# First attention of a two-layer block: rotary exchange by DMA instead of a second projection, and the maxima in two groups of two

## The reference, cut to what matters

```python
# H, KV, DH = 16, 4, 64 ; G = 4 query heads share one key/value head
def _rotate_half(t):
    t1, t2 = t[..., :DH // 2], t[..., DH // 2:]
    return concatenate([-t2, t1], axis=-1)
q = (x @ Wq).reshape(B, L, H, DH); k = (x @ Wk)...; v = (x @ Wv)...
q = q * cos + _rotate_half(q) * sin
k = k * cos + _rotate_half(k) * sin
attn = softmax(einsum("bqkgd,bskd->bkgqs", qg, k) * DH ** -0.5)
out = einsum("bkgqs,bskd->bqkgd", attn, v).reshape(B, L, H * DH) @ Wo
```

## Time and profile before

| | us |
|---|---|
| median of 3 runs (1546.03 to 1549.05) | 1546.24 |
| the profiled execution, its own time | 1553.07 |
| its span, from first to last instruction | 1551.1 |
| first attention, from its first DMA to its last score tile | 37 to about 860 |
| a whole sequence of eight steps in the loop | 96.7 |

### The profile page before, as it was taken

How to read it: one execution, slowest core, us unless ns; L and a number is a source line. 1 busy time by engine, 2 the same in 40 slices (tenths; PEclk the granted TensorE clock), 3 DMA queues, 4 the chain that set the end, 5 groups by cost and what they waited for, 6 DMA issues and landing times. The chain is left out here.

```text
span 1551.1 us, 29838 instructions
## 1 busy us (share of the span) xinstructions
PE 1149.9 (74%) x10864; PEld 718.6 (46%) x10864; DVE 1105.2 (71%) x1557; ACT 608.0 (39%) x1176; POOL 841.0 (54%) x772
## 2 busy tenths in 40 slices
PE   2388999989999899999999436555448886165554
PEld 1135565645655556556565424333214676133343
DVE  2377978868789588797878458986227775469983
ACT  1134545545455354564546123332124330133331
POOL 0267878869788597987979213331026564023320
PEclk9578999999999899999999858988655898668896
DMA  2221212212121121221211000000000000000001
GB/s 69 74 43 43 43 33 53 43 31 49 34 55 37 24 63 33 53 43 22 63 33 33 15 0 1 0 0 1 14 11 1 1 1 1 14 0 0 1 0 55
DMA packets 48100, 42.17 MB, mean 27 GB/s; under 512 B 7734, under 2 KB 46154, under 8 KB 47946
## 3 DMA queue, kind: packets, MB, share of 16 engines
q1 hardware_dynamic: 47946, 40.14, 11.4%
HBM read 6.42 MB, written 2.10 MB: 5 GB/s over the span
## 5 line engine op out<-in xcount | busy, mean ns | idle before, releaser
L661 POOL TENSOR_TENSOR a_p_lo<-a_probs 128x512 f16<-128x512 f32 x384 | 418.6, 1113 | 29.1 <-ACT a_probs L515 25.3
L515 ACT ACTIVATE a_probs<-a_ps_s 128x512 f32<-128x512 f32 x512 | 304.0, 597 | 327.2 <-PE a_ps_s L447 322.7
L597 DVE TENSOR_REDUCE a_nmx<-a_ps_m 128x2 f32<-128x1024 f32 x256 | 311.0, 1216 | 33.4 <-PE a_ps_m L430 32.6
L463 PE MATMUL a_ps_o<-a_v_hi,a_probs 128*128 128x65 f16 x2048 | 243.0, 196 | 7.6 <-POOL a_p_lo L661 7.6
L464 PE MATMUL a_ps_o<-a_v_lo,a_probs 128*128 128x64 f16 x2048 | 240.3, 194 | 0.0
L465 PE MATMUL a_ps_o<-a_v_hi,a_p_lo 128*128 128x65 f16 x2048 | 240.0, 194 | 0.0
L463 PEld LDWEIGHTS a_ps_o<-a_v_hi,a_probs 128*128 128x128 bf16 x2048 | 189.3, 98 | 79.1 <-issue 48.5
L445 PE MATMUL a_ps_s<-a_qq,a_kk 128*128 128x512 f16 x512 | 198.0, 387 | 10.4 <-issue 6.2
L464 PEld LDWEIGHTS a_ps_o<-a_v_lo,a_probs 128*128 128x128 bf16 x2048 | 191.1, 99 | 25.1 <-issue 1.0
L447 PE MATMUL a_ps_s<-a_qq,a_k_l 65*128 65x512 f16 x512 | 198.6, 388 | 0.0
L465 PEld LDWEIGHTS a_ps_o<-a_v_hi,a_p_lo 128*128 128x128 f16 x2048 | 190.9, 98 | 0.0
(11 more groups left out here) (218 smaller groups left out, 2105.9 us busy)
## 6 DMA issues: line engine op xcount, KB each, us to landing
a_qq<-a_rhi SPq DMA_DIRECT2D x128, 128.0 KB, 2.4
a_qq<-a_rlo SPq DMA_DIRECT2D x128, 64.0 KB, 2.1
a_kk<-a_rhi SPq DMA_DIRECT2D x64, 64.0 KB, 2.0
a_k_l<-a_rlo SPq DMA_DIRECT2D x32, 64.0 KB, 2.0
out_x<-x_sb SPq DMA_DIRECT2D x1, 2048.0 KB, 8.7
a_qq<-a_nmT SPq DMA_DIRECT2D x64, 2.0 KB
m_w<-in_wmod SPq DMA_DIRECT2D x2, 384.0 KB
a_probs<-in_wq SPq DMA_DIRECT2D x1, 512.0 KB, 3.7
```

The lines of the kernel that those rows point to most:

```text
L463: nc.tensor.matmul(out, hi, v_hi[:, b % 2, kt, g, 0:65], start=(kt == 0), stop=False)
L515: nc.scalar.activation(probs[:, p % 2, kt, h, :], ps_s[:, i % 2, :], ACT.Exp, scale=DH0 ** -0.5).then_inc(exp_done, 1)
L597: nc.vector.tensor_reduce(nmx[:, p % 2, i:2 * QT:QT], ps_m[:, n % 2, :, :], axis=X, op=ALU.max, negate=True).then_inc(free[n % 2], 1)
L661: nc.gpsimd.tensor_tensor(p_lo[:, p % 2, kt, h, :], pr, pr.bitcast(BF16)[:, 1:2 * L:2], ALU.subtract).then_inc(lo_pool, 1)
```

## The change

The second projection is dropped. `A` and `K` are now three matmuls in one bank; DVE reads that bank twice (a broadcast) and writes q cos and q sin. The sine product is then exchanged 32 partitions by 32 by four SBUF-to-SBUF DMAs of 64 KB each (new items `RD` and `KD`, issued by SP), and POOL's `RS` waits for them. The projection moves from three to four pairs ahead and from slot 1 to slot 6, with `RD` in slot 7; the four maximum jobs move from slots 0, 2, 4, 6 to 1, 1, 5, 5; `O` from slot 3 to slot 2; the key rope is spread over two steps; DVE's share of `L` moves from tiles 2 and 6 to tiles 3 and 7. The set-up loses the eight weight copies (L556).

```diff
-        if pair(s + 2):
-            for i in range(4):
-                slots[2 * i].append(("B", s + 2, i))
+        if pair(s + 4):
+            slots[6].append(("A", s + 4))
+            slots[7].append(("RD", s + 4))
         if pair(s + 3):
-            slots[1].append(("A", s + 3))
             slots[3].append(("RS", s + 3))
             slots[4].append(("RH", s + 3))
             slots[5].append(("RL", s + 3))
+        if pair(s + 2):
+            for i in range(4):
+                slots[1 + 4 * (i // 2)].append(("B", s + 2, i))
...
         if pair(s - 2):
-            slots[3].append(("O", s - 2))
+            slots[2].append(("O", s - 2))
...
         if (b := seq(-5)) is not None:
             for m in range(2):
                 slots[2 + 3 * m].append(("K", b, m))
-                slots[4 + 2 * m].append(("KS", b, m))
-                slots[5 + 2 * m].append(("KH", b, m))
-                slots[6 + m].append(("KL", b, m))
+                slots[3 + 3 * m].append(("KD", b, m))
+            slots[7].append(("KS", b, 0))
         if (b := seq(-4)) is not None:
+            slots[0].append(("KH", b, 0))
+            slots[1].append(("KL", b, 0))
+            slots[1].append(("KS", b, 1))
+            slots[2].append(("KH", b, 1))
+            slots[3].insert(0, ("KL", b, 1))
             slots[5].append(("V", b))
...
-        LO_DVE, LO_POOL = (2, 6), (0, 1, 3, 4, 5, 7)
+        LO_DVE, LO_POOL = (3, 7), (0, 1, 2, 4, 5, 6)
...
+                if kind in ("RD", "KD"):
+                    key = it[1:]
+                    r = rope[key]
+                    t.jobs(free, job[("A" if kind == "RD" else "K",) + key], 1)
+                    for k in range(4):
+                        src, dst = slice(32 * k, 32 * (k + 1)), slice(32 * (k ^ 1), 32 * (k ^ 1) + 32)
+                        sp.dma_start(rsw[dst, r % NR, :], rcs[src, r % NR, 1, :]).then_inc(rope_swap[r % NR], 16)
...
-                    for swap in range(2):
-                        out = ps_m[:, n % 2, swap, :]
-                        hi, lo = (w[:, swap, j * 128:(j + 1) * 128] for w in (w_hi, w_lo))
-                        nc.tensor.matmul(out, hi, hT_hi[:, b % 2, :], start=True, stop=False)
-                        nc.tensor.matmul(out, hi, hT_lo[:, b % 2, :], start=False, stop=False)
-                        last = nc.tensor.matmul(out, lo, hT_hi[:, b % 2, :], start=False, stop=True)
+                    hi, lo = (w[:, j * 128:(j + 1) * 128] for w in (w_hi, w_lo))
+                    nc.tensor.matmul(bank, hi, hT_hi[:, b % 2, :], start=True, stop=False)
+                    nc.tensor.matmul(bank, hi, hT_lo[:, b % 2, :], start=False, stop=False)
+                    last = nc.tensor.matmul(bank, lo, hT_hi[:, b % 2, :], start=False, stop=True)
...
-                    t.ropes(rope_sum, r - 1, 1)
-                    nc.vector.tensor_tensor(rcs[:, r % 2, :, :], ps_m[:, n % 2, :, :], cossin[:],
+                    t.ropes(rope_sum, r - NR + 1, 1)
+                    nc.vector.tensor_tensor(rcs[:, r % NR, :, :], ps_m[:, n % 2, 0:1, :].to_broadcast([128, 2, L]), cossin[:],
                                             ALU.mult).then_inc(free[n % 2], 1)
...
-                    t.jobs(free, job[("A" if kind == "RS" else "K",) + key], 1)
+                    t.wait(rope_swap[r % NR], (r // NR + 1) * 64, ROPE16 // NR * 64)
                     t.ropes(rope_lo, r - 1, 1)
-                    nc.gpsimd.tensor_tensor(rot[:, r % 2, :], rcs[:, r % 2, 0, :], rcs[:, r % 2, 1, :],
+                    nc.gpsimd.tensor_tensor(rot[:, r % 2, :], rcs[:, r % NR, 0, :], rsw[:, r % NR, :],
                                             ALU.add).then_inc(rope_sum, 1)
```

More of the change, by code:

```diff
@@ L201, in layer0_attention @@
     ROPE16 = rope[(LOOP_FROM + 3 + PERIOD,)] - rope[(LOOP_FROM + 3,)]
-    assert JOBS16 % 2 == 0 and ROPE16 % 2 == 0
+    assert JOBS16 % 2 == 0 and ROPE16 % NR == 0
     with ExitStack() as ex:
@@ L212, in sem @@
             return ex.enter_context(nc.semaphore(f"a0_{name}"))
[L215 to L218, removed]
+        wq_hi = sb("wq_hi", [D, H0 * DH0], FP16)
+        wq_lo = sb("wq_lo", [D, H0 * DH0], FP16)
+        wk_hi = sb("wk_hi", [D, KV0 * DH0], FP16)
+        wk_lo = sb("wk_lo", [D, KV0 * DH0], FP16)
         wv_hi = sb("wv_hi", [D, KV0 * DH0], FP16)
@@ L234, in layer0_attention @@
         hT_lo = sb("hT_lo", [D, 2, L], FP16)
-        rcs = sb("rcs", [128, 2, 2, L])
+        rcs = sb("rcs", [128, NR, 2, L])
+        rsw = sb("rsw", [128, NR, L])
         rot = sb("rot", [128, 2, L])
@@ L265, in layer0_attention @@
         loaded, ready = sem("loaded"), sem("ready")
-        swapped, w_hi_done = sem("swapped"), sem("whi")
+        split, w_hi_done = sem("split"), sem("whi")
+        rope_swap = [sem(f"rswap{k}") for k in range(NR)]
         full = [sem("full0"), sem("full1")]
@@ L357, in item @@
                 kind = it[0]
-                if kind == "RL":
+                if kind in ("RD", "KD"):
[5 more added lines that the diff above has]
+                        sp.dma_start(rsw[dst, r % NR, :], rcs[src, r % NR, 1, :]).then_inc(rope_swap[r % NR], 16)
+                elif kind == "RL":
                     p, r, sl = it[1], rope[it[1:]], it[1] % 4
@@ L387, in _ @@
             pe.wait_ge(ready, 5)
-            pe.wait_ge(swapped, 1)
+            pe.wait_ge(split, 1)
             def item(t, it):
@@ L487, in _ @@
             nc.scalar.activation(ident16[:], ident[:], ACT.Copy).then_inc(ready, 1)
-            for whole, hi in ((wq, wq_hi[:, 0, :]), (wk, wk_hi[:, 0, :]), (wv, wv_hi[:])):
+            for whole, hi in ((wq, wq_hi[:]), (wk, wk_hi[:]), (wv, wv_hi[:])):
                 nc.scalar.activation(hi, whole, ACT.Copy, scale=WSCALE).then_inc(w_hi_done, 1)
@@ L547, in _ @@
             dve.wait_ge(w_hi_done, 3)
[L548 to L557, removed]
+            for whole, hi, lo in ((wq, wq_hi[:], wq_lo[:]), (wk, wk_hi[:], wk_lo[:]), (wv, wv_hi[:], wv_lo[:])):
+                last = nc.vector.scalar_tensor_tensor(out=lo, in0=whole, scalar=WSCALE, in1=hi, op0=ALU.mult,
+                                                      op1=ALU.subtract)
+            last.then_inc(split, 1)
             def item(t, it):
@@ L1549, in tables @@
     sin = np.sin(emb).T.astype(np.float32) / np.float32(WSCALE)
-    sin[:DH0 // 2] *= -1
+    sin[DH0 // 2:] *= -1
     sin = np.tile(sin, (2, 1))
```

## The result

The change makes the kernel slower: 1611.68 us median (1608.64 to 1614.08, 4 runs) against 1546.93 for the kernel before, measured again beside it; ratio 1.0415, 95% interval 1.0393 to 1.0438. The forecast was 1592 (1550 to 1622), slower. The profiled execution of the changed kernel took 1612.8 us, its span is 1611.0, so 59.9 us more span than the 1551.1 of before.

What follows compares the result with a forecast made beforehand. PE was taken to bound the kernel, a closed chain through SP after the change. Plain steps +22, K and V +21, W -8, start +12, last steps -1: +46 on 1546.24 gives 1592 us, range 1550 to 1622.

Steps and rivals of the forecast that it cites:

- The bound of before: Plain steps before the change: PE sets the pace, busy 41.6 of 42 us, DVE 38.3, POOL 37.1.
- the most that this edit can give: PE: three of six matmuls fewer per rope, 0.64 us each over 80 ropes, 51 us of PE work.
- first rival: SP's exchange issues take at most 0.55 us each and stay hidden; plain step 9.75, total 1516 us; 10%.
- What is removed: PE loses 0.64 us per rope; DVE's product stays at 1.22 us, reading one bank twice priced at nothing; weight copies -1.2 us.
- The four issues and the chain: Plain steps: RS, L, RL, q issues, exchange issues, landing, next RS close a 10.8 us chain against 10.13; +0.7 each, +22.
- K and V: K and V steps: 38 SP issues nearly without pause, 29.2 us against 26.2; +3.0 a sequence, +21 in all.
- W: Output projection lets DMAs catch up; with the plain step before it, -1.2 us a sequence, -8 in all.
- Start: Before the loop no attention covers the chain: first K issue at 67.4, RS of pair 2 at 99; +12 us.
- Last steps: Steps at the end have no rope and one bank wait less: -1 us.
- The sum: All terms together +46 us on the median 1546.24, giving 1592 us; the forecast's own range 1565 to 1617.
- The second: Rival: exchange issues, with only 32 rows, take 0.43 us, not 0.64; gains and losses cancel, about 1546 us; 9%.
- The third: Rival: PE's granted clock falls too after waits in the V step, 25 us on top of +46: 1617 us; 13%.

Runs made afterwards that it cites:

- the ladder above: Medians from the kernel before, 1546 us: new order of work alone 1572, then second projection dropped without exchange 1534, then exchange added (the change) 1612.

## Why the prediction was right, and where not

**The bound of before** held: with PE as the bound, 0.64 us less PE work had to show in each plain step once nothing else held it, and it did, 10.49 to 9.85 between the two kernels that differ in the second projection alone. But the 51 us called "the most that this edit can give" came to 38, and the new order of work took 26 of them back. For a plain step the prediction has of this only an estimate of 0.25 us, in its first rival; 0.36 was measured, and in the change itself it is hidden under the chain.

**What is removed**: L582's successor takes 1.215 us on 75 of its executions, from a bank read twice, as against 1.22: the zero for the broadcast was right.

**The four issues and the chain** held, link by link. Means of the 28 turns from RS to RS in plain steps, with the forecast in brackets: 3.71 us from RS to the first q issue (3.5), 5.04 to the last exchange issue (4.65 and 0.5 for long issues), 2.29 to the next RS (2.12); together 11.03 (10.8). Six and two issues in place of four moved the plain step up 1.6 and down 1.0, and reversing the order on SP opened the chain. The term mis-sized is L between RS and RL: I took its mean of 1.11, but DVE's share of L now falls beside it in 17 of the 28 turns, and it takes 1.49 us then and 1.04 otherwise. DVE's product, RD's other condition, came after the q issues in 3 turns. So +0.81 a plain step and not +0.7.

**K and V** took 30.1 us against 29.2 forecast. On the table's ruler that is +3.17, but the forecast added its +3.0 to 26.2, the figure of one sequence, and on its own ruler, from RS to RS, seven times K and V give +27.1 and not +21. The reason was right only in part. I laid it all on 38 SP issues; the ladder above gives 2.3 of the 3.17 to the exchange, and 0.9 went when the key rope stood in one step again (27.8 to 26.9 without the exchange). What holds the remaining 26.9, with four projections' halves less to do on PE than before, stays open.

**W**: the forecast's -8 is for the step before W and W together; from RS to RS, over seven sequences, the two gave -8.3. (The -7.6 of the table is the W steps alone.) Half of it is the order of work: with the double projection and the new slots the W steps of the table are 4.1 us shorter already.

**Start**: +12.3 against +12, and its links too: the first K issue at 68.1 (67.4 forecast), RS of pair 2 at 99.4 (99). **Last steps**: +1.1 in the four of them against -1. And +4.0 us lie behind the first attention, for which the prediction had no term; they are within the spread between profiles (690 to 701), and nothing ties them to the edit.

**The sum**: +59.9 us of span, +64.8 between medians, against +46. The forecast case's own range, up to 1617, held it. From RS to RS the plain distances gave +27 and not +22, K and V +27 and not +21; what follows the last RS gave +3.3 and not -1. A further 5 us of the 64.8 is no step at all: the profiled execution of the kernel before lay 6 us above its median, that of the change 1.

**The rivals.** The first, the exchange hidden at 0.55 us an issue, had nearly the right floor for a plain step (9.75 against 9.85 measured), the wrong one for K and V (27.8). It fell with its condition: two issues more made a turn 1.31 us longer, 0.65 each. The Trainium skill, DMA: Bandwidth & Descriptors, Anatomy of one DMA, gives about 50 ns for the sequencer's dispatch, on the gpsimd path; carried over to SP that figure isn't borne out, by the same 0.65 us. The second fell with the first, as the exchange's issues took 0.6 like all others. The third came true in its first half: the granted clock over K and V is 0.80 to 0.89 in all seven sequences, where before it was 1.00 in five and fell to 0.91 and 0.89 only in the two behind the loop's jump back. The same steps as in the row of 0.89 above, before:

```profile
427.00:454.00 27.00, 25.16 (x301) 14.33 (x299) 20.17 (x26) 14.61 (x28) 24.52 (x22) 1.00 0.27 58
```

So PE ran part of them at 1.2 GHz after its waits. What that cost was not separated; it can be part of the 0.9 us by which K and V exceed their forecast. Without the exchange, too, the clock over K and V was 0.83 to 0.94.

## What to carry to other kernels

Look for closed chains before looking at leads: if one iteration's transfer is issued behind something that waits for the previous iteration's transfer, its length is a floor on the iteration. That no projection further ahead changes this was argued and not run; that the order on the issuing queue does, was. Nor did any run issue the exchange from another engine. Price a DMA by its issue on the queue that issues it, here 0.6 to 0.7 us for transfers within SBUF from 2 to 128 KB, so merge transfers by laying the data out (here neighbours and not halves) before moving them about. And where jobs take two banks in turn, a move of one job by one slot is a new neighbour two jobs back; check who reads that bank, and how long.

## What was not expected of the hardware

A 128 KB exchange with every second partition as source and as destination landed in 2.1 us, a 64 KB one with 32 neighbouring partitions in 2.0; its issue was no dearer either (two in 1.17 us). Stride over partitions and twice the bytes together cost 0.1 us of landing and nothing in the issue.

POOL's L took 1.04 us at most in the 266 cases of the changed kernel in which DVE ran no L beside it, and 1.27 in the mean, up to 1.55, in the 118 in which it did. DVE's maxima beside it made no such difference.

The stages behind the first attention, the same instructions in all these kernels, took from 690 to 701 us in the profiled executions, at a mean granted clock of 0.75 to 0.77, while the 35 plain steps of the first attention lay within 0.13 us of each other in the kernel before and within 0.05 in the one with O alone back in slot 3 (10.01 to 10.06).
